# Residual of the attention stage summed in PSUM by an identity product, with the sum copied out by ScalarE

## What is computed

```python
def _L3_conv_ref(x, Wq, Wk, Wv, gamma):          # called with x = _gn(x3)
    xf = x.reshape(b, c, h * w)
    f = jnp.einsum('oc,bcn->bon', Wq, xf)
    g = jnp.einsum('oc,bcn->bon', Wk, xf)
    hh = jnp.einsum('oc,bcn->bon', Wv, xf)
    scores = jnp.einsum('bki,bkj->bij', f, g)
    beta = jax.nn.softmax(scores, axis=1)
    o = jnp.einsum('bci,bij->bcj', hh, beta)
    out = gamma[0] * o + xf
...
x4 = x3 + _L3_conv_ref(_gn(x3), ...)
```

## Time and profile before

| | us |
|---|---|
| median of three runs | 2304.32 |
| lowest and highest | 2300.87, 2311.59 |
| profiled execution, its time | 2306.92 |
| profiled execution, its span | 2305.0 |

### The profile page before, as it was taken

How to read it: one execution, slowest core, us unless ns; L and a number is a source line. 1 busy time by engine, 2 the same in 40 slices (tenths; PEclk the granted TensorE clock), 3 DMA queues, 4 the chain that set the end, 5 groups by cost and what they waited for, 6 DMA issues and landing times. The chain is left out here.

```text
span 2305.0 us, 40585 instructions
## 1 busy us (share of the span) xinstructions
PE 1888.4 (82%) x15572; PEld 1215.3 (53%) x15572; DVE 1408.7 (61%) x2847; ACT 898.2 (39%) x2181; POOL 274.6 (12%) x77
## 2 busy tenths in 40 slices
PE   2799999999999999778778999994377776876768
PEld 1355555566666665566656677762134443444446
DVE  4676677765555554322222455554899989999984
ACT  0444444444444445333333444441123333233332
POOL 1000000000000000000000000001243434434340
PEclk9899999999999999899888999997578888887879
DMA  2122322375657656888878665642112112121101
GB/s 96 46 81 71 105 71 77 113 197 171 188 166 215 187 163 165 191 222 217 214 220 218 164 153 160 156 113 74 42 42 70 46 54 70 57 68 56 59 28 43
DMA packets 264469, 279.45 MB, mean 121 GB/s; under 512 B 208788, under 2 KB 234772, under 8 KB 264280
## 3 DMA queue, kind: packets, MB, share of 16 engines
q1 hardware_dynamic: 264120, 276.59, 42.8%
q0 software_dynamic: 160, 0.26, 0.0%
HBM read 161.21 MB, written 115.61 MB: 120 GB/s over the span
## 5 line engine op out<-in xcount | busy, mean ns | idle before, releaser
L484 DVE TENSOR_TENSOR vk<-p_vk,mask_vo 128x512 f32<-128x512 f32 x256 | 176.8, 691 | 556.7 <-PE p_vk L378 556.7
L1449 POOL TENSOR_TENSOR rstd<-var,minus_half 128x32 f32<-128x32 f32 x32 | 173.9, 5433 | 1896.3 <-DVE var L1025 1896.3
L414 PE MATMUL p_dw<-tw,qd 98*64 98x98 f32 x3072 | 244.0, 295 | 90.7 <-ACT agg_out L627 63.2
L414 PEld LDWEIGHTS p_dw<-tw,qd 98*64 98x64 f32 x3072 | 200.4, 206 | 154.7 <-ACT agg_out L627 80.7
L627 ACT ACTIVATE agg_out<-p_dw 128x294 f32<-128x294 f32 x256 | 106.4, 416 | 332.2 <-PE p_dw L414 254.0
L600 ACT ACTIVATE half_b<-p_qkv 98x384 f32<-98x384 f32 x256 | 125.2, 489 | 233.6 <-PE p_qkv L337 231.7
L437 PE MATMUL p_g<-o,w_proj 128*128 128x392 f32 x512 | 206.5, 529 | 3.0 <-DVE var L540 2.4
L337 PE MATMUL p_qkv<-w_qkv,half_a 128*98 128x384 f32 x512 | 190.8, 496 | 6.7 <-DVE half_a L556 6.7
L337 PE MATMUL p_qkv<-w_qkv,z_odd 128*98 128x384 f32 x512 | 190.4, 495 | 1.8 <-DVE z_odd L556 1.8
L390 PE MATMUL p_out<-vk,qr 128*49 128x136 f32 x2048 | 173.6, 291 | 1.0 <-DVE oN L499 1.0
L635 ACT ACTIVATE o<-p_turn 128x196 f32<-128x196 f32 x256 | 85.2, 333 | 163.0 <-PE p_turn L399 162.1
(11 more groups left out here) (176 smaller groups left out, 3191.4 us busy)
## 6 DMA issues: line engine op xcount, KB each, us to landing
qkv_scratch<-half_b SPq DMA_DIRECT2D x32, 1176.0 KB
qd<-qkv_scratch SPq DMA_DIRECT2D x64, 588.0 KB
agg_scratch<-agg_out SPq DMA_DIRECT2D x128, 294.0 KB, 5.5
tw<-in_w_toep SPq DMA_DIRECT2D x128, 220.5 KB
x_scratch<-xb SPq DMA_DIRECT2D x32, 784.0 KB, 5.2
half_a<-agg_scratch SPq DMA_DIRECT2D x48, 392.0 KB, 6.9
half_b<-agg_scratch SPq DMA_DIRECT2D x48, 392.0 KB, 6.7
half_a<-in_x SPq DMA_DIRECT2D x16, 784.0 KB, 4.8
```

The source lines that it names most:

```text
L414: mm = pe.matmul(p_dw[NP * cp:NP * cp + NP, PR * s:PR * s + PR], qd[:, QB % 2, :, ch - QB_CH * qb], tw[:, SB % 2, :, 6 * (F % SB_FILLS) + ...
L484: v.tensor_tensor(dst[:, :, 0:128].rearrange("p k (c n) -> p k c n", c=HC), src[:, :, 0:2 * D].unsqueeze(2).to_broadcast([128, 4, HC, 2 * D]),
L1449: done(g.tensor_tensor(rstd[k][:, :, :].rearrange("p t b -> p (t b)"), var[k][:, :], W["minus_half"][:, :], ALU.pow), f"rstd{k + 2}")
```

## The change

In `pe_out` a second identity product adds the slice of x3 to the same PSUM tile, right after the one with z3, for each m and each half. The addition `v_x4` is gone from VectorE. In its place ScalarE runs `a_x4`, a plain copy of the PSUM tile to x4, with the same waits and the same semaphore `x4_ok`. For m = 0 it stands after `a_beta` and before `a_sums`, for m = 1 first in the next body, before `a_fg`.

```diff
--- before.py
+++ after.py
@@ -1165,14 +1165,6 @@
             done(v.scalar_tensor_tensor(sc[:, :, :, :], sc[:, :, :, :], W["gamma"][0:PR, 0:1], over(srec[:, :, :]),
                                         ALU.mult, ALU.mult), "probs")
 
-        def v_x4(v, it, m):
-            wait(v, "o_mm", 4 * it + 2 * m + 2)
-            if m == 0:
-
-                wait(v, "stored", 16 * it)
-            done(v.tensor_tensor(by_half(x4[:, m, :]), (p_a, p_b)[m][:, :, 0:HALF], by_half(x3[it % 3][:, m, :]),
-                                 ALU.add), "x4_ok")
-
         def v_body(v, intake, norm2, gate, norm3, attend, leave):
 
             def run(step, chunk, *more):
@@ -1181,7 +1173,6 @@
 
             run(v_sum, norm3, 1)
             run(v_hot, gate)
-            run(v_x4, leave, 1)
             run(v_mean, norm3, 1)
             run(v_mean, norm2, 0)
             run(v_centre, norm3, 1)
@@ -1203,7 +1194,6 @@
             run(v_scale, norm2, 0)
             run(v_gap, norm2)
             run(v_scale, norm3, 1)
-            run(v_x4, attend, 0)
 
 
         def pe_stat(pe, it, k, n):
@@ -1319,6 +1309,8 @@
                 wait(pe, "bt_ev", 2 * it + h + 1)
                 pe.matmul((p_a, p_b)[m][:, h, 0:HALF], W["ident"][:, :], z3[it % 2][:, m, HALF * h:HALF * h + HALF],
                           start=True, stop=False)
+                pe.matmul((p_a, p_b)[m][:, h, 0:HALF], W["ident"][:, :], x3[it % 3][:, m, HALF * h:HALF * h + HALF],
+                          start=False, stop=False)
                 for q in range(4):
                     mm = pe.matmul((p_a, p_b)[m][:, h, PR * q:PR * q + PR],
                                    hh[:, 4 * h + q, 128 * m:128 * m + 128], beta[:, h, q, :],
@@ -1360,6 +1352,13 @@
             wait(a, f"centred{k + 2}", it + 1)
             done(a.activation(sq[k][:, :, :], zc[k][:, :, :], ACT.Square), f"squared{k + 2}")
 
+        def a_x4(a, it, m):
+            wait(a, "o_mm", 4 * it + 2 * m + 2)
+            if m == 0:
+
+                wait(a, "stored", 16 * it)
+            done(a.activation(by_half(x4[:, m, :]), (p_a, p_b)[m][:, :, 0:HALF], ACT.Copy), "x4_ok")
+
         def a_sums(a, it):
             wait(a, "s_mm", it + 1)
             done(a.activation(s_sb[:, :], p_group[0:GR, 0, 0:HALF], ACT.Copy), "s_ev")
@@ -1422,6 +1421,7 @@
                 if chunk is not None:
                     step(a, chunk, *more)
 
+            run(a_x4, leave, 1)
             run(a_fg, attend)
             run(a_gap, gate)
             run(a_square, norm3, 1)
@@ -1435,6 +1435,7 @@
             run(a_tanh, gate)
             run(a_hh, attend, 3)
             run(a_beta, attend)
+            run(a_x4, attend, 0)
             run(a_sums, norm2)
 
 
```

## The result

The changed kernel takes 2357.43 us (median of four runs, 2356.57 to 2369.95), beside 2306.47 us for the kernel before. The ratio is 1.0235, 95% interval 1.0199 to 1.0272. It counts a fifth run of the changed kernel, of 2361.68 us, and lies a little over the ratio of the two medians. The forecast was 2351 us, +46.7 us on the 2304.3 us of the kernel before. The medians lie 51 us apart; the ratio makes it 54 us, which is 2360.7 us on the median of before, just above the top of the forecast's range, 2360. So the sign and the place were forecast, and the size a few us too small.

A forecast was written before the change was run, and what follows sets the result against it. Last-phase bodies were taken as bound by TensorE for some 18.7 us and by VectorE with its helpers for some 22.3. Twelve longer bodies (+35.8 us) and four last output stages (+10.9) made +46.7, so 2351 us, range 2341 to 2360.

The forecast's parts named there:

- term (d): Clock rise after the gate in each last-phase body: may come later with longer bodies, a late rise costing 1 us.
- best place: Clock rising as early as in the settled bodies of before: 40.96 + 2.72 = 43.68 us per body.
- What bounds: Last-phase body: TensorE bounds some 18.7 us from gate product to statistics, VectorE with its helpers some 22.3 us.
- R2: Rival: VectorE is the bound, so removing its additions saves 31 us, time 2273 us; 5 in 100.
- (a): Two VectorE additions per chunk go, 1.93 us per body, worth nothing as VectorE waits on TensorE there.
- The sign given for it: VectorE's wait before L1001 was to grow from 1.6 to about 6 us.
- (b): Four x3 identity products per chunk between turn and statistics, 0.68 us each, 2.72 us per chunk, none hidden.
- (c): Two ScalarE copies out of PSUM per chunk, about 0.92 us each, free because later work's inputs come later.
- R4: Rival: a copy delays L1365 or L1394 by 0.35 us per body, bodies 45.0, time 2362 us; 10 in 100.
- The end: Last four output stages, led by TensorE: 4 x 2.72 = +10.9 us; a final addition of 0.97 becomes a 0.92 copy.
- The sum: Twelve bodies at 44.2 us (+35.8) and four last output stages (+10.9) give +46.7, so 2351 us.
- R3: Rival: gate and values run warm, 2.6 us per body comes back, no change to speak of, 2306 us; 5 in 100.

The follow-up runs named there:

- e1: The changed kernel without its four identity products of x3 per chunk, so the output lacks x3: 2308.12 us against 2309.79 for the kernel before, ratio 0.9991.
- e2: The kernel before with only the four identity products added, VectorE still adding x3, so x3 counts twice: 2355.97 us, ratio 1.0199 to before.
- e3: The changed kernel with the x3 products for m = 0 only, two instead of four per chunk: 2335.65 us, ratio 1.0116 to before.
- e9: The complete changed kernel in a second new order, TensorE's sums and both statistics ahead of work VectorE doesn't wait for, ScalarE following: 2301.87 us, 0.9982 to before.
- e7: The kernel before with z3 + x3 summed beforehand by POOL, no identity product, VectorE adding the sum to PSUM: 2314.72 us, ratio 1.0019 to before.
- e6: The changed kernel with z3 + x3 summed beforehand by POOL and one identity product instead of two: 2313.49 us, ratio 0.9997 to before.
- e8: The changed kernel with the order of e5 together with the POOL sum and single identity product of e6: 2404.2 us, ratio 1.0398 to before.
- e5: The complete changed kernel in a first new order, statistics, gap and hot products before the m = 1 output product and projections: 2372.72 us, ratio 1.0260 to before.
- e12: e9 with ScalarE's square for the gate ahead of its third copy of the values instead of behind it: 2274.4 us, ratio 0.9836 to before.

## Why the prediction was right on the cause, and which term was short

The cause, the place and the sign came as forecast. The step that failed is term (d), what the clock adds to a body. The forecast put 44.2 us on each of the twelve bodies, 0.52 above its own best place; they average 44.43 us, 0.83 above the sum of before and products. With the measured bodies the forecast's own sum gives 2353.7 us, which is inside its range. That the 2360.7 us by the ratio lie just over the top of it comes from this term, from a body that the sum left out (0.8 us), from the median of before, 2.2 us higher here than the one forecast from, and from the spread of the runs.

- **What bounds.** Right. The stretch from the gate product to the statistics is TensorE's, and VectorE waits at L1001. e1 shows it from the one side (1.93 us taken off VectorE, no gain), e2 from the other (the products alone give the whole loss). R2 is excluded by both.
- **(a), the removed additions at nothing.** Right. The sign given for it, about 6 us of wait before L1001, came as two waits: 4.39 us there and 2.52 us at L1056, since the additions no longer cover the wait for the sums. Together with TensorE's 3.2 us they hold the 1.93 us that the additions had taken.
- **(b), four products at 0.68 us.** 0.66 us each, all four in the chain: 2.64 us instead of 2.72. None was hidden, and in the settled body none fell into the stretch at 0.50.
- **(c), the copies at nothing.** Right. They take 0.83 us, not 0.92: the slope between 392 and 512 columns was too steep to carry on to 784. The Trainium skill, ScalarE: Activation LUTs, section What ACT_TABLE_LOAD costs, gives 0.84 us by its formula, an estimate, and this trace agrees with 0.82 to 0.83. ScalarE is idle for 0.62 us between the copy of p_a and L1364 and for 0.66 us between that of p_b and L1393, so no queue formed and R4 fails.
- **(d), the clock.** Mis-sized. The twelve bodies take 533.12 us and average 44.43; the settled ones at 44.37 stand 0.77 us above the sum of before and products, where the forecast had added 0.52, and those before them reach 44.73. By the measured products that is 0.83 us per body for the clock, 3.7 us more in twelve bodies than forecast; products of 0.66 instead of 0.68 us take 1.0 off. What is left is 2.7 us, 38.5 against 35.8.
- **The end.** Four stages at 2.72, +10.9: from the last gate product of those twelve bodies to the end of the span it is 2368.1 - 2256.46 = 111.64 us against 2305.0 - 2204.20 = 100.80, +10.8. That it fits so well is partly luck: the first body in it is 3.23 us longer (42.29 us where it was 39.06), the three stages behind it are 2.5 us longer each.
- **The sum.** 38.5 + 10.8 = 49.3 us where 46.7 were forecast. The body before the first output stage adds 0.8 us (37.31 us from gate to gate at a mean granted clock of 0.64, where it was 36.51 at 0.73, and 36.52 at 0.73 in e2 with the same products), and the two stretches before it give back 0.4: +49.7 in all. The medians' 51 us leave 1.3 us that no trace places. The range was cut too narrow at the top: its upper end allowed for 56 us, and the ratio's interval reaches from 46 to 63 us. R3 fails: the stretch from gate into the values is at 0.50 in every body seen.

What stays open: why a body settles where it does. The runs show that the same work takes some 0.8 us more or less with the place of the rise (e3 has both side by side, e2 has 43.57 and 44.37 us), and that two, four and six products give one, two and three kinds of bodies in some turn. That the longer bodies follow from the place of the rise, rather than both from a third thing, is argued from the values that run longer, not shown by an edit of the clock alone.

## What to carry to other kernels

Ask of each engine's work not how much it is but who waits behind it. In the first order TensorE's queue held back the statistics that VectorE waits for, and four products cost 50 us; in e9 VectorE waits for TensorE nowhere in a body, and they cost nothing in the bodies. Relieving an engine pays only where it is last, and there it may need the other engines' queues put in another order first; then follow the wait from one line to the next until it is gone, since it moved twice here (L1001, L1025, L1121) before the body was VectorE's own. When TensorE runs part of each body at 0.50 and the work in the body grows, give what the clock adds a range as wide as all the bodies seen; here the middle was too low.

## What the runs showed of the hardware that was not expected

- The bodies don't settle on one length: with two products they alternate between 42.28 and 43.05 us, with six they turn through 44.99, 46.03 and 45.51 us, with the rise of the clock in a different place of each.
- An f32 addition of two SBUF tiles on POOL (L1464, 128x1568, 3.5 us) held up a `tensor_tensor` of VectorE with both inputs in SBUF that started during it (L1059, 64x392, else 0.56 us). One body of e7:

```profile
2068.57 3.51 POOL L1464 TENSOR_TENSOR x<-x,z 128x1568 f32<-128x1568 f32 x1
2069.00 3.50 DVE L1059 TENSOR_TENSOR hot<-s_sb,best 64x392 f32<-64x392 f32 x1
```

- In e6, e7 and e8 L1059 lasted from 2.1 to 3.7 us in such bodies, by how early it had started, and always ended 0.42 us after POOL's addition. VectorE's additions out of PSUM (L1174 of e7, one input in PSUM) that started during the same addition of POOL took 0.97 to 0.98 us, as elsewhere, and its reductions beside POOL's other product (4.3 us) kept their 1.78 us.
- A new order comes with another granted clock: e5 and e8 were granted 0.75 and 0.71 in their longest bodies, where a settled body of the changed kernel has 0.85 and one of e12 0.91. How much of the loss of e5 and e8 is the clock and how much the wait at L1025 wasn't separated.
